# The order of the first loads and the first statistics in an adaLN block with a state-space and a channel-mixing half

## The reference, cut to what matters

```python
mod = (_silu(c) @ wmod).reshape(16, 6, 1, -1)
sa, ca, ga, sb, cb, gb = ...                      # shift, scale, gate; gates kept away from 0
h = _layernorm(x) * (1 + ca) + sa
x = x + ga * ssm(h)                               # first half
h = _layernorm(x) * (1 + cb) + sb
x = x + gb * channel_mix(h)                       # second half

# ssm: u, gate = split(h @ W_in.T); dt = softplus(u @ W_dt.T + b); b = u @ W_state.T
#      state scan over the 512 tokens; y = state @ W_C.T
#      out = (y * silu(gate) + h * D) @ W_out.T
# channel_mix: token shift, r = sigmoid(xr @ W_r.T), k = relu(xk @ W_k.T)**2, out = r * (k @ W_v.T)
```

## Time and profile before

| | |
|---|---|
| runs shown | 343.62, 343.72 and 874.88 us, median 343.72 |
| the profiled execution | 343.59 us |
| its span, first to last instruction | 341.8 us |
| busy shares of the span | PE 98%, DVE 89%, ACT 86%, POOL 81% |
| bytes moved | 36.00 MB, 105 GB/s in the mean |

### The profile page before, as it was taken

One profiled execution on the slowest core, in us unless ns is written; L12 is line 12 of the kernel. 1 busy time (PEld: TensorE's weight loads), 2 busy tenths in 40 slices (PEclk: granted clock), 3 DMA queues, 4 the chain that ended last, 5 costly groups with the idle time before them and its releaser, 6 DMA issues.

```text
span 341.8 us, 5185 instructions
## 1 busy us (share of the span) xinstructions
PE 335.0 (98%) x1574; PEld 265.4 (78%) x1574; DVE 303.6 (89%) x465; ACT 292.4 (86%) x393; POOL 275.5 (81%) x274
## 2 busy tenths in 40 slices
PE   8999998999999999999999999999999999999995
PEld 4567676788888888888888888888888888887764
DVE  3789888999999999999999999999999989887846
ACT  4486778989999999999999998999999999888484
POOL 2151879989898998989899898989899896966752
PEclk9999999999999999999999999999999999999999
DMA  7960523060513406051421505151320501010013
GB/s 276 416 226 13 172 83 104 1 221 27 186 61 112 136 18 221 11 186 63 161 85 64 186 0 186 63 186 61 102 83 14 174 3 61 1 63 0 2 60 126
DMA packets 18556, 36.00 MB, mean 105 GB/s; under 512 B 4960, under 2 KB 5728, under 8 KB 18400
## 3 DMA queue, kind: packets, MB, share of 16 engines
q1 hardware_dynamic: 17808, 35.19, 29.7%
q10 hardware_dynamic: 720, 0.48, 0.5%
HBM read 27.22 MB, written 8.44 MB: 104 GB/s over the span
## 4 chain that ended last, share of the span: by engine, by line
PE 89%; DVE 5%; issue 3%; ACT 2%; POOL 0%; DVEq 0%; ACTq 0%; POOLq 0%
PE slot L293 71%; PE slot L386 4%; PE slot L300 4%; PE slot L537 2%; PE slot L528 2%; PE slot L527 2%; PE slot L307 1%; PE slot L314 1%; PE slot L333 1%; DVE xk L979 1%; DVE xr L979 1%; DVE xn L945 1%; PE slot L394 1%; DVE h L940 0%; ACT prev L663 0%
## 5 line engine op out<-in xcount | busy, mean ns | idle before, releaser
L1173 POOL TENSOR_TENSOR k_lo<-k_act,k_hi 128x512 fp32r<-128x512 f32 x30 | 50.2, 1694 | 4.5 <-ACT k_act L872 4.5
L663 ACT ACTIVATE prev<-slot,mod,mix_prev 128x512 f32<-128x512 f32 x64 | 46.4, 785 | 1.3 <-PE slot L300 0.7
L293 PE MATMUL slot<-h_hi,wf_hi 128*128 128x512 f32 x120 | 43.0, 399 | 0.1
L1173 POOL TENSOR_TENSOR xr_lo<-xr,xr_hi 128x512 fp32r<-128x512 f32 x32 | 42.7, 1337 | 0.2 <-ACT xr_hi L709 0.2
L293 PE MATMUL slot<-h_hi,wf_lo 128*128 128x512 f32 x120 | 41.9, 390 | 0.0
L1173 POOL TENSOR_TENSOR xk_lo<-xk,xk_hi 128x512 fp32r<-128x512 f32 x30 | 38.6, 1315 | 3.7 <-ACT xk_hi L703 3.7
L1232 POOL TENSOR_TENSOR h_lo<-h,h_hi 128x512 fp32r<-128x512 f32 x28 | 36.5, 1305 | 1.3 <-ACT h_hi L684 1.3
L1294 POOL TENSOR_TENSOR z_lo<-z,z_hi 128x512 fp32r<-128x512 f32 x26 | 33.3, 1303 | 2.7 <-ACT z_hi L858 2.7
L293 PE MATMUL slot<-h_lo,wf_hi 128*128 128x512 f32 x120 | 34.2, 389 | 0.0
L979 DVE SCALAR_TENSOR_TENSOR xk<-slot,mix_new,prev 128x512 f32<-128x512 f32 x32 | 23.8, 746 | 8.2 <-issue 7.9
L945 DVE TENSOR_SCALAR xn<-slot,stats,rstd 128x256 f32<-128x256 f32 x62 | 29.2, 532 | 0.0
(11 more groups left out here) (164 smaller groups left out, 977.6 us busy)
## 6 DMA issues: line engine op xcount, KB each, us to landing
x_ch<-x_ch_in SPq DMA_DIRECT2D x16, 512.0 KB, 4.3
x_tok<-x_tok_in SPq DMA_DIRECT2D x15, 512.0 KB, 5.4
x_out<-wmod SPq DMA_DIRECT2D x15, 512.0 KB, 3.2
spread_rows<-rows_spread SPq DMA_DIRECT2D x13, 512.0 KB, 3.8
wmod<-wmod_in SPq DMA_DIRECT2D x1, 1024.0 KB, 8.5
w_in<-weights_in SPq DMA_DIRECT2D x1, 1024.0 KB, 11.2
w_in<-weights_in SPq DMA_DIRECT2D x1, 512.0 KB, 4.5
wmod<-wmod_in SPq DMA_DIRECT2D x1, 512.0 KB, 5.8
```

Source lines behind the costliest of these rows:

```text
L293: ins = nc.tensor.matmul(out, w[:, c, at + d * P:at + (d + 1) * P], x[:, c, :], start=first, stop=last)
L663: return nc.scalar.activation(prev[:, mix, i, 1:T + 1], ps_n[:, i, :], ACT.Identity, bias=mod_at(SHIFT2 + i, k), scale=mix_prev[:, mix, i, ...
L1173: nc.gpsimd.tensor_tensor(lo, x, hi.bitcast(F32), ALU.subtract).then_inc(done, 1)
```

## The change

Two things are changed, both for sequence 0 alone. In SyncE's queue the request for the front weights goes ahead of that for the first half of the first tokens; everything behind keeps its place. And VectorE takes the statistics of tiles 2 and 3 first, waiting for the half that ScalarE asked for, and then those of tiles 0 and 1, waiting for SyncE's half. The semaphore that marks the end of the statistics is still raised by the last of the four, now that of tile 1.

```diff
-            sp.dma_start(x_tok[:, 0, 0:TT // 2], x_tok_d[0, :, 0:TT // 2]).then_inc(s_xt[0], 16)
             w_early_d = w_d[:, 0:CH * 3 * C].rearrange("p (c n) -> p c n", c=CH)
             sp.dma_start(w_early[:, :, 0:GATE], w_early_d[:, :, 0:GATE]).then_inc(s_w, 16)
+            sp.dma_start(x_tok[:, 0, 0:TT // 2], x_tok_d[0, :, 0:TT // 2]).then_inc(s_xt[0], 16)
             wmod_cols = wmod_d.rearrange("(c p) n -> p c n", p=P)
...
             def ln1_stats(k):
-                dve.wait_ge(s_xt[k % 3], 16 * (k // 3 + 1))
-                for t in range(TT):
-                    if k == 0 and t == TT // 2:
-                        dve.wait_ge(s_xt0, 16)
+                if k == 0:
+                    dve.wait_ge(s_xt0, 16)
+                else:
+                    dve.wait_ge(s_xt[k % 3], 16 * (k // 3 + 1))
+                for t in range(TT) if k > 0 else (2, 3, 0, 1):
+                    if k == 0 and t == 0:
+                        dve.wait_ge(s_xt[0], 16)
                     last = nc.vector.bn_stats(stats1[:, k % 2, t, :], x_tok[:, k % 3, t, :])
```

## The result

| | before | changed |
|---|---|---|
| runs | 9, 343.44 to 344.24 and one of 874.88 | 9, 344.45 to 345.86 and one of 485.61 |
| median | 344.02 us | 344.60 us |
| ratio | | 1.0026, 95% interval 1.0015 to 1.0037 |

The account below looks back on a forecast made before the run. The prediction took TensorE's chain to be the bound, so only the first h matmul's start counted. Terms of 0 (weights) and 1.08 - 0.68 = +0.40 us (tokens) on 343.59 gave 344.0 us, range 343.4 to 344.8.

Parts of the forecast that it names:

- What bounds the kernel: TensorE carries 89% of the chain; any microsecond before the first h matmul at 10.98 us is one of the whole.
- Part one: Front weights land near 4.8, not 5.66, but warming matmuls and modulation weights hide it: term 0, bounds -0.06 to 0.
- Part two: The first token half, now second in SyncE's queue, lands at 5.66, 1.74 us later; bounds 5.24 and 7.43.
- the two queues share the engines about equally: Read from the two 256 KB token halves, one per queue, landing together at about 4.0 us; used for the weights' landing.
- the forecast's own formula: Late half's landing plus its pair of statistics, less their old end of 5.38 and the slack, gives the delay: +0.40 us.
- Part three: On VectorE the early pair of statistics is hidden, the late pair takes 0.74 us; statistics end at 6.46, 1.08 later.
- The sum: 1.08 - 0.68 = +0.40 us at the transposes, the first h matmul (10.98 to 11.38) and the end; 344.0 us.
- slack of 0.68: Time the token chain could be late before TensorE's transposes: 9.21 - 8.47 - 0.06 = 0.68 us.
- The delay in the slack: Rival: the late token half lands by 5.26, its chain ends by 9.15, nothing moves: 343.6 us; chance 0.22.
- Faster: Rival: modulation weights land 0.2 earlier and the half before 5.1, so the fold's gain passes on: 343.4 us; chance 0.05.
- Much slower by a late half: Rival: the half trails into the modulation weights behind a lagging DMA engine; at 6.3 +1.04, 344.6 us; chance 0.14.
- The clock drop: Rival: TensorE's pause before the transposes lowers its clock for the twelve h matmuls: +5.4, 349.4 us; chance 0.01.

Follow-up runs that it names:

- e1: The changed kernel run again without edit, for a profile; 344.43 against 344.05 us, profiled execution 344.52 us.
- e13: The kernel before with the tensor of packed token halves among its inputs but not read; 344.03 against 344.09 us, ratio 0.9995.
- e2: The kernel before with only the two requests exchanged, statistics in the old order; 345.20 against 344.05 us, ratio 1.0044.
- e14: The changed kernel with the tensor of packed token halves among its inputs but not read; 344.55 against 344.09 us, ratio 1.0030.
- e11: The kernel before with each half of the first tokens laid out as a 256 KB block of its own; 344.10 us, ratio 1.0017.
- e15: A repetition of e11, the kernel before with the token halves apart; one run of 344.13 us.
- e4: The kernel before with the changed statistics order, the second pair also waiting for the front weights; 343.92 against 344.05 us, ratio 0.9996.
- e3: The kernel before with only the statistics exchanged, requests in the old order; 343.68 us, ratio 0.9990.
- the first two comparisons: Changed kernel against the one before: first the runs of the result table, ratio 1.0026, then 12 runs against 35 on one chip, ratio 1.0009.
- the third: Comparison of the changed kernel with the one before, with an unread tensor among the inputs (e14); 344.55 against 344.09 us, ratio 1.0030.
- e5: The changed kernel with each queue beginning with 256 KB of front weights, each followed by a token half; 346.00 against 343.96 us, ratio 1.0045.
- e6: The kernel before with SyncE asking for weights, then both token halves, ScalarE only for small ones; old statistics; 346.07 us, ratio 1.0054.
- e7: The kernel before with modulation weights ahead of front weights, and TensorE doing modulation first, then fold and transposes by halves; 346.80 against 343.96 us.
- e8: The kernel before run once more without edit, for a second profile; 343.37 us.
- e12: The kernel before with the front weights and the first modulation weights each as a tensor of its own; 346.41 us, ratio 1.0053.
- e9: The changed kernel with the front weights as a tensor of their own; 346.22 against 344.12 us, ratio 1.0058.

## Why the prediction was right or wrong

**What bounds the kernel.** Right. The difference between the profiles before and after (e1) stands ahead of the first h matmul and is handed on whole: 0.90 there, 0.93 at the end. What doesn't hold is that a granted clock of 0.998 hides no slow clock: e13 reads 0.999 and e1 0.999, with folds of 2.78 and 2.83 us.

**Part one: nothing to win from earlier weights.** Right in its result, wrong in its reason. The weights didn't land near 4.8 but at 5.52, within the 5.46 to 5.66 of before's requests, so there was no gain to hide and the warming matmuls had nothing to do. The modulation weights, forecast at 7.43 "with the same bytes ahead", landed at 7.70 in e1 and at 7.62 in e2 and e14; with 7.03 to 7.83 in the profiles of before's requests this is neither a confirmation nor a loss, but the bounds of -0.06 to 0 were far narrower than that spread. In e2, with a fast fold, their arrival held the modulation (first load 7.65), but the tokens hid it.

**Part two: the late half lands at 5.66.** This is the step that failed. That the half has "just the bytes that the weights had", and so lands where they did, sized the delay at 1.74 us; it was 2.38 (3.92 to 6.30; landings of 6.22 in e2 and e14). Within SyncE's queue all landed in the order of asking. What isn't the same is the pace of the first bytes: with the two halves of the same rows at the head 336 GB/s were moved from 2 to 3 us in e13, and with the weights beside one of the halves 195 in e1 and e14. ScalarE's half suffered as well, 5.23 instead of the forecast's unchanged 4.13, so "the two queues share the engines about equally" didn't carry over from before. The landings of the earlier trace rows were taken as a rate of the DMA engines, while they also held the pair that was under way together; e11 and e15 show that the layout of this pair alone moves them by up to 1 us. Why the memory is read faster in one arrangement than in the other stays open. With the measured 6.30 in the forecast's own formula: 6.30 + 0.80 - 5.38 - 0.68 = 1.04, against the 0.90 found; the rest of the formula was thus 0.14 too dear in e1, and 0.10 in e4.

**Part three: the order of the statistics.** Right: 0.75 for the late pair, the early one hidden (5.28 to 6.03 in e1, over 1 us later than forecast, with 0.27 us to spare), and e3 shows no cost by itself. Without it the change would have cost 0.6 us more (e2 against e1).

**The sum.** The mechanism (late half, token chain, slack of 0.68, h matmuls) is shown by e4, which made 11.28 where the forecast for this delay was 11.38. The size was off by the landing: +0.40 forecast, +0.93 between the profiles, and 0.95 to 1.01 between the quickest executions, where e4, with the delay that was forecast, has +0.38. The time of 344.60 lies inside the range because the range took in late landings, up to about 6.4. That the medians are only 0.38 to 0.58 apart, near the forecast's 0.40, is luck, and comes from the spread of before. 343.59 is an execution with an early clock. When the clock is late, the kernel before loses up to 0.9 us itself (e13, 344.28), and the changed kernel, whose modulation may be late up to the tokens at 10.09, loses next to nothing more: e1 had the slow fold, and its twelve runs stand between 344.28 and 344.76, those of before between 343.33 and 344.53, apart from four. Late tokens and a late clock aren't added; the later of them counts. That would hide e4's 0.38 in its median too. Of the 0.60 us between the forecast of 344.0 and 344.60, 0.30 lie in the baseline, a median of 343.72 over three runs that became 344.02 over nine. That the first two comparisons gave 0.26% and 0.09% has in part another cause, the clock drops described next: two of eight runs of the changed kernel in the first and none in the second, none of before's in the first and four of 35 in the second. Without them the means are 0.70 and 0.50 us apart, and 0.44 in the third.

**The rivals.** The delay in the slack: no, the half was 1 us past the point that it named. Faster: no, the modulation weights didn't land 0.2 earlier (7.62 to 7.70), and the half not before 5.1. Much slower by a late half, given 0.14: its numbers (landing at 6.3, 344.6 us) are what was measured. Whether its cause took part, one engine that trails behind the others, isn't known, since no view here parts the 16 engines; from 2 to 3 us their mean share was 0.79 in e1 against 0.99 in e13. The clock drop, given 0.01: it does occur. The stretches of e5's profile show the granted clock (third column from the end):

```profile
9.00:11.00 2.00, 0.79 (x8) 0.72 (x8) 1.62 (x6) 0.62 (x2) 0.51 (x2) 1.00 1.04 423
...
12.00:13.00 1.00, 1.00 (x3) 0.50 (x2) 0.97 (x3) 0.73 (x2) 0.00 (x0) 0.50 1.11 459
13.00:14.00 1.00, 1.00 (x2) 0.34 (x1) 0.93 (x5) 0.00 (x0) 0.00 (x0) 0.50 1.02 430
...
15.00:16.00 1.00, 1.00 (x4) 0.44 (x3) 0.23 (x1) 0.51 (x1) 0.00 (x0) 1.00 0.95 373
```

TensorE had been idle for 1.21 us ahead of the transposes, then the clock stood at the lower level of 1.2 GHz from about 11.5 to 14.5, and the twelve h matmuls took longer than their 5.39:

```profile
10.55 1.14 PE slot L407 x8
11.69 0.85 PE slot L315 x2
12.54 6.34 PE slot L294 x12
```

It costs about 1.3 us in all, not 5.4: runs of e2 with a mean clock of 1.000 or 0.998 took 344.95 to 345.26, those of 0.993 or 0.995 took 346.21 to 346.61. The changed kernel had two such runs of eight in the first comparison (345.73, 345.86), none of twelve in the second, and three of eight in e14; the kernel before had six of 113 over all comparisons (four of 35, two of 29, and none of 8, 26 and 15). With the longer pauses of e2, e5 and e6 it is about half of the runs or more (5 of 12, 6 of 9, 7 of 10). That a longer pause makes it more frequent is what these counts suggest; how it is set off wasn't tried by itself. Not every long run is such a drop: two of e11 (346.01 and 345.94) and most long ones of e7 show a mean clock of 0.999 or 1.000.

## What to carry to other kernels

A landing time read from a trace belongs to the pair of transfers that were under way together; when a change breaks up such a pair, "the same bytes ahead" is an estimate, and its bound has to leave room on the late side (here 0.56 to 0.64 us more than the row of the same size). Before paying for an earlier operand, look at what the engine does just before it and at the operand after it: here the modulation weights and the tokens were due within a microsecond, and exchanging two requests could only move the wait. A change of a few tenths of a microsecond is better read from where one instruction starts in several profiles, and from the quickest executions, than from medians, when executions of one kernel are spread over a whole microsecond.

## What the runs showed of the hardware

- Two queues that read neighbouring 2 KB pieces of the same 4 KB rows at once delivered 512 KB by 3.93 to 4.33 us (before, e3, e4, e7, e8, e12, e13). The same amount in two contiguous blocks apart took until 4.93 and 4.73 (e11, e15), and 512 KB of weights in one queue until 4.62 (e6). What in the memory makes the difference is open, and so is whether it is the neighbourhood or the contiguous layout.
- Laying 512 KB of weights in one piece made them later behind the tokens (6.57 against 5.66 us, e12 against before) and a little earlier at the head (5.32 against 5.52, e9 against e1), where ScalarE's half beside them came at 3.33 instead of 5.23. The cause wasn't looked for.
- The fold of eight matmuls took 1.99 us (e8) to 2.78 (e13) with the same code and order of loads, and 2.83 in e1. Its weight loads took 0.19 us in e8 and up to 0.34 in e1, the times that e5 has at granted clocks of 1.00 and 0.50; the column of the granted clock reads 1.00 over both folds.
- In e5 the granted clock stood at 0.50 from 12 to 14 us, after an idle 1.21 us ahead of the transposes; executions of e2 with a mean clock of 0.993 or 0.995 were about 1.3 us longer than its others.
